# Keys, embedding and last norm turned by VectorE in 32x32 squares and moved between partitions by DMA through DRAM

## The chip, the cores and the metric

The kernel runs on one core of a Trainium2 chip. The metric is the device time of one execution in microseconds. All values are float32; matrix products are made of float32r pieces, each operand being split into a high part and a low part (the rest), with three products for one.

## What is computed

Eight samples of 512 tokens with 256 channels go through one gated block: an attention-free layer with a band of position biases, a two-layer network with 1024 hidden channels, and a gated token-shift network.

```python
def xattn(x, pos, wq, bq, wk, bk, wv, bv, wo, bo, pos_bias, gamma, beta, w1, b1, w2, b2):
    emb = x + pos
    q, k, v = emb @ wq + bq, emb @ wk + bk, emb @ wv + bv
    w = pos_bias * (abs(i - j) < 64)
    ek, ew = exp(k - max_over_tokens(k)), exp(w - max_of_row(w))
    y = sigmoid(q) * (ew @ (ek * v)) / (ew @ ek)
    a = layer_norm(y @ wo + bo + emb) * gamma + beta
    return layer_norm(relu(a @ w1 + b1) @ w2 + b2 + a) * gamma + beta
def ffn(x, W_r, W_k, W_v, mu_r, mu_k):          # x_prev is x moved by one token
    xr, xk = mu_r * x + (1 - mu_r) * x_prev, mu_k * x + (1 - mu_k) * x_prev
    return sigmoid(xr @ W_r.T) * (square(relu(xk @ W_k.T)) @ W_v.T)
x = x + tanh(g_xattn) * xattn(norm(x), ctx, ...)
x = x + tanh(g_ffn) * ffn(norm(x), ...)          # norm(x) here is "the last norm"
```

## The kernel before

Weights stay in SBUF. A sample is worked on in two layouts: rows (128 tokens on the partitions, four tiles of 256 channels) and channels (128 channels on the partitions, two chunks of 512 tokens). Three tensors per sample change layout on TensorE, with eight 128x128 transposes each, into PSUM:

- the embedding `emb`, rows to channels (`turn_emb`, L1444), for keys, queries and values. ScalarE takes the high part from PSUM (`emb_high`, L1097), VectorE the low part (`emb_low`, L588);
- the exponentials of the keys `ek_t` (the buffer of `y`), channels to rows (`turn_keys`, L1468), for the weighing by the band. ScalarE makes the high part (`ek_high`, L1114), VectorE the low part (`keys_low`, L634) and the product with the values (`weigh_values`, L639), both from PSUM;
- the last norm, rows to channels (`turn_fin`, L1599), which ScalarE copies to `xn_t` (`turned_copy`, L1131).

A fourth turn, of the middle norm, is not touched. The work is a software pipeline. `run_steps` (L303) writes out steps 1 to 7 for every engine. In step i four samples are in work: i in the attention and the first hidden chunks, b = i-1 in the last hidden chunks and the sum, a = i-2 in the token-shift network, d = i+1 in embedding, keys, queries and values; e = i+2 is being loaded and normed. Each engine has its own order written by hand in its `step` (SyncE L392, GpSimd L508, VectorE L879, ScalarE L1253, TensorE L1695), and an instruction waits for semaphores, with everything behind it on its engine. There is no planner.

In TensorE's step the order is: the weighing of the keys (`weigh`, part 0), the embedding's turn for d, the weighing of the values with a hidden chunk inside, `ffn_k` of a, keys of d, `ffn_r`, hidden chunks 2 and 3 of b with the output projection between, `ffn_v`, sums of the second layer, the middle norm's turn, queries of d, hidden chunks 0 and 1 of i, values of d, the keys' turn, a sum of the second layer, and the last norm's turn for b. VectorE begins with `sums_low`, the first reciprocal, `sums_low` again, the mix `xk` of a, `emb_low`, the second reciprocal and the mix `xr`. SyncE's queue holds in each step the second load of x, loads of x and the context for e, and the store of a. TensorE begins a step only with `ek_hi` and `val` of that sample.

GpSimd makes the low parts of `xr` and `y` and adds a row to `emb` in between (`xr_low`, `emb_plus_bo`, `y_low`). ScalarE's `exp_keys` of d writes the buffer of `y`, so it waits for `y_low`, and `hidden_high` of b's chunk 2 comes behind it.

Of the kernel before, what the change touches and what calls it, by code (L numbers as in the profile page):

```python
# [1 line left out]

# [24 lines left out]
FIN_DVE = 3  # L27
FIRST_DVE = 2
NU = 8

# [17 lines left out]
def flamingo_gated_block(nc, A_x, A_ctx, A_vec, A_rows, A_far, A_pos, A_wk, A_wq, A_wv, A_wo,  # L48
# [14 lines left out]
    with ctx:  # L63
# [82 lines left out]
        def pair(k):  # L146
# [52 lines left out]
                                                                   sem("sq_lo_done"), sem("tanh_r_done"))  # L199
        gated_done, out_done = sem("gated_done"), sem("out_done")  # L200
        last_norm_dve, last_sq_lo = sem("last_norm_dve"), sem("last_sq_lo")

# [38 lines left out]
        def sq_low(eng, n):  # L241
            low(eng, sq_lo, xk, sq_hi, sq_hi_done, n + 1, sq_lo_done)

        def make_emb(eng, n, p):
# [103 lines left out]
        def _(sp):  # L348
# [16 lines left out]
            def store(n):  # L365
                sp.wait_ge(out_done, n + 1)
                sp.dma_start(rows_of(out, n), out_sb.rearrange("p (b a d) -> p b a d", b=1, a=TT)).then_inc(out_stored, 16)

            load_x(0)
            load_ctx(0, 0)  # L370
# [41 lines left out]
        def _(pool):  # L412
# [43 lines left out]
            def emb_plus_bo(n, p):  # L456
                pool.wait_ge(emb_turned, n + 1)
                pool.wait_ge(rows_landed, 16 * 6)
                add_row(emb[p], bo_rows, emb_bo_done)
# [48 lines left out]
            def step(i, p):  # L508
# [19 lines left out]
                if has(e):  # L528
                    make_emb(pool, e, p)
                stats("ff", b)  # L530
                stats("fin", b)

            run_steps(pool, step)
# [33 lines left out]
        def _(dve):  # L567
# [71 lines left out]
            def weigh_values(n):  # L639

                dve.wait_ge(val_done, n + 1)
                dve.tensor_tensor(val, pair(0), val, ALU.mult).then_inc(ev_done, 1)

# [17 lines left out]
            def recip(n, c):  # L661

                dve.wait_ge(den_done, DC * n + c + 1)
                dve.wait_ge(exp_q_done, DC * n + c + 1)
                if c == 0:
                    dve.wait_ge(ek_turned, n + 1)
# [75 lines left out]
            def mix_k(n, chunks=range(DC)):  # L742

                mixed(n, xk, C_MUK, xk_done, chunks)

            def mix_r(n, chunks=range(DC)):

                mixed(n, xr, C_MUR, xr_done, chunks)

# [129 lines left out]
            def step(i, p):  # L879
# [25 lines left out]
                hidden_low(b, 3)  # L905
                if is_last(i):
                    normalise_mid(i)
                if has(a):
                    gate_ffn(a)
                if not is_last(i):  # L910
                    normalise_mid(i)
                if has(a):
                    make_out(a)
# [3 lines left out]
                ff_stats(b, None if is_last(i) else lambda: a_low(i))  # L917
                scale_ff(b)
                finish_x1(b)
                fin_stats(b)  # L920
# [3 lines left out]
                if has(d):  # L924
                    keep_values(d)
                    keys_low(d)
                    weigh_values(d)
# [139 lines left out]
        def _(act):  # L1067
# [29 lines left out]
            def emb_high(n):  # L1097
                act.wait_ge(emb_turned, n + 1)
                act.activation(emb_hi, pair(0), ACT.Copy).then_inc(emb_hi_done, 1)  # L1099

# [13 lines left out]
            def ek_high(n):  # L1114
                act.wait_ge(ek_turned, n + 1)
                after(act, wo_done, n)
                act.activation(ek_hi, pair(0), ACT.Copy).then_inc(ek_hi_done, 1)

# [12 lines left out]
            def turned_copy(n):  # L1131
                after(act, xr_done, DC * n)
                for c in range(DC):
                    o = c * (T + 1) + 1
                    act.wait_ge(fin_turned, DC * n + c + 1)
                    act.activation(xn_t[:, o:o + T], bank(2, c), ACT.Copy).then_inc(xn_t_done, 1)

# [115 lines left out]
            def step(i, p):  # L1253
                a, b, d, e = i - 2, i - 1, i + 1, i + 2
                if has(d):
                    after(act, v_done, d)
                    emb_high(d)
# [27 lines left out]
                if has(d):  # L1285
                    ek_high(d)
                if not is_last(i):
                    turned_copy(b)
                if has(d):
# [69 lines left out]
        def _(pe):  # L1359
# [122 lines left out]
            def weigh(n, part, dst, hi, lo, lo_ready, done, between=None, ahead=None):  # L1482

                near(dst, 0, hi, (ew_hi, ew_lo), True)
                if part == 0:
                    pe.wait_ge(lo_ready, n + 1)
                    near(dst, 0, lo, (ew_hi,))
                    after(pe, xn_t_done, DC * (n - 1))
                    relus_read(NQ * (n - 1) + 2)
# [205 lines left out]
            def step(i, p):  # L1695
# [3 lines left out]
                weigh(i, 0, 1, ek_hi, ek_lo, ek_lo_done, den_done)  # L1699
                if has(d):  # L1700
                    turn_emb(d, 1 - p)
# [42 lines left out]
                if has(d):  # L1744
                    values(d)
                    turn_keys(d)
                if not is_last(i):
                    add_hidden(i, 0)
                    turn_fin(b)

# [141 lines left out]
```

## Time and profile before

| | us |
|---|---|
| three runs | 475.52, 475.59 (median), 478.38 |
| profiled execution, whole | 477.9 |
| its span | 476.2 |
| TensorE matmuls busy | 453.5 |
| VectorE busy | 391.8 |
| ScalarE busy | 239.6 |
| GpSimd busy | 259.4 |
| granted TensorE clock, mean | 0.996 of full speed |

Busy time counts instructions of an engine while they run, by the profiler's records; the span is the time from the first to the last of them, and the profiled execution's own time has a little around it. In the rows PE is TensorE, DVE VectorE, ACT ScalarE, POOL GpSimd and SP SyncE; an L-number is a line of the kernel before. Matmuls overlap in the pipeline, so the time that a group of them takes is read from the starts of neighbours, not from their durations.

### The profile page before, as it was taken

The page shows a single profiled execution, that of the slowest core. Times are in us where ns is not written, and L with a number is a line of the kernel's source. Part 1 is how long each engine was busy: PE and PEld are TensorE (multiplying, and loading weights), DVE is VectorE, ACT ScalarE, POOL GpSimd, SP SyncE. Part 2 cuts the span into 40 slices and gives each one's busy share as a digit, 9 for nine tenths or more (in the row PEclk, how much of TensorE's full clock was granted, in tenths as well). Part 3 has the DMA queues.
Part 4 walks back from the last instruction along what each step waited for, and adds up shares of the span by engine and source line. Part 5 has one row for each costly group of instructions (what it writes and reads, how often), then busy time and mean ns, then how long its engine had stood idle before and what let it go on. Part 6 is the DMA issues. An engine that isn't in the chain of part 4 may idle for free.

```text
span 476.2 us, 8229 instructions
## 1 busy us (share of the span) xinstructions
PE 453.5 (95%) x3080; PEld 412.4 (87%) x3080; DVE 391.8 (82%) x733; ACT 239.6 (50%) x372; POOL 259.4 (54%) x239
## 2 busy tenths in 40 slices
PE   7889989899999999999999999999999999999975
PEld 7779788779989898999989898899989898897975
DVE  4898879986959989598968989599867979489987
ACT  3582562645265634736356643735345543538253
POOL 2574843661587535971577634973567335953621
PEclk9999999989999999999999999999999999999999
DMA  8740410102001300022001210021000110011002
GB/s 265 267 132 8 144 50 2 44 12 79 1 1 63 114 3 0 1 89 89 1 1 45 94 41 1 1 89 44 1 2 0 51 39 1 1 45 45 2 0 89
DMA packets 21895, 23.35 MB, mean 49 GB/s; under 512 B 992, under 2 KB 20960, under 8 KB 21856
## 3 DMA queue, kind: packets, MB, share of 16 engines
q1 hardware_dynamic: 20768, 21.26, 13.7%
q10 hardware_dynamic: 1088, 1.57, 1.0%
q8 instruction: 24, 0.39, 0.3%
q14 instruction: 15, 0.12, 0.1%
HBM read 18.64 MB, written 4.19 MB: 48 GB/s over the span
## 4 chain that ended last, share of the span: by engine, by line
PE 43%; issue 19%; POOL 16%; DVE 14%; ACT 4%; DMA 2%; ACTq 0%; POOLq 0%; DVEq 0%
PE ps L1361 40%; DVE y L670 4%; POOL xk_lo L225 3%; POOL hid_lo L225 3%; PE ps L1367 2%; POOL a_rows L434 2%; DMA hid<-in_wo 2%; DVE xk L738 1%; PE ps L1376 1%; POOL emb L434 1%; POOL ek_lo L225 1%; POOL ev_lo L225 1%; POOL x_beta L434 1%; DVE y L667 1%; DVE hid_lo L814 1%
## 5 line engine op out<-in xcount | busy, mean ns | idle before, releaser
L1361 PE MATMUL ps<-w_hi,hid_hi 128*128 128x256 f32 x288 | 72.2, 288 | 0.8 <-issue 0.5
L1361 PE MATMUL ps<-w_lo,hid_hi 128*128 128x256 f32 x288 | 70.6, 281 | 0.0
L814 DVE SCALAR_TENSOR_TENSOR hid_lo<-ps,neg_b,hid 128x512 fp32r<-128x512 f32 x60 | 41.3, 739 | 34.5 <-ACT hid L1190 34.5
L1361 PEld LDWEIGHTS ps<-w_hi,hid_hi 128*128 128x128 f32 x288 | 54.2, 188 | 3.5 <-DVE y L677 2.2
L1361 PEld LDWEIGHTS ps<-w_lo,hid_hi 128*128 128x128 f32 x288 | 54.3, 189 | 0.1
L670 DVE RECIPROCAL y<-y 128x512 f32<-128x512 f32 x16 | 53.7, 3353 | 0.6
L1361 PE MATMUL ps<-a_hi,w_hi 128*128 128x512 f32 x128 | 50.8, 397 | 1.1 <-DVE hid_lo L814 1.1
L1361 PE MATMUL ps<-a_hi,w_lo 128*128 128x512 f32 x128 | 50.7, 396 | 0.0
L1184 ACT ACTIVATE hid_hi<-ps,b 128x512 fp32r<-128x512 f32 x60 | 37.9, 686 | 24.8 <-PE ps L1361 24.8
L225 POOL TENSOR_TENSOR ev_lo<-res,ev_hi 128x1024 fp32r<-128x1024 f32 x8 | 19.1, 2383 | 51.7 <-ACT ev_hi L1129 51.7
L1361 PE MATMUL ps<-w_hi,hid_lo 128*128 128x256 f32 x288 | 41.6, 284 | 3.4 <-DVE hid_lo L814 2.2
L1361 PEld LDWEIGHTS ps<-w_hi,hid_lo 128*128 128x128 f32 x288 | 37.1, 188 | 4.8 <-DVE hid_lo L814 2.4
L1190 ACT ACTIVATE hid<-hid_hi,neg_b 128x512 f32<-128x512 f32 x60 | 40.1, 725 | 0.0
L1361 PE MATMUL ps<-a_lo,w_hi 128*128 128x512 f32 x128 | 35.1, 396 | 0.0
L434 POOL TENSOR_TENSOR a_rows<-norm,gamma_rows 128x1024 f32<-128x1024 f32 x8 | 20.1, 2509 | 19.7 <-issue 17.3
L1361 PEld LDWEIGHTS ps<-a_hi,w_hi 128*128 128x128 f32 x128 | 24.0, 188 | 6.7 <-DVE hid_lo L814 1.6
L225 POOL TENSOR_TENSOR xk_lo<-xk,xk_hi 128x1024 fp32r<-128x1024 f32 x7 | 17.2, 2460 | 22.6 <-ACT xk_hi L1141 22.6
L1361 PEld LDWEIGHTS ps<-a_lo,w_hi 128*128 128x128 f32 x128 | 24.1, 188 | 5.8
L1361 PEld LDWEIGHTS ps<-a_hi,w_lo 128*128 128x128 f32 x128 | 24.1, 189 | 5.2
L1361 PE MATMUL ps<-emb_hi,w_hi 128*128 128x512 f32 x64 | 26.9, 420 | 0.5 <-ACT emb_hi L1099 0.5
L1361 PE MATMUL ps<-emb_hi,w_lo 128*128 128x512 f32 x64 | 25.6, 399 | 0.0
L225 POOL TENSOR_TENSOR hid_lo<-xr,hid_hi 128x1024 fp32r<-128x1024 f32 x5 | 12.1, 2410 | 22.5 <-ACT hid_hi L1148 22.5
(251 smaller groups left out, 1327.5 us busy)
## 6 DMA issues: line engine op xcount, KB each, us to landing
x_in<-in_x SPq DMA_DIRECT2D x8, 512.0 KB, 4.4
emb<-in_ctx SPq DMA_DIRECT2D x8, 512.0 KB, 3.5
x_beta<-in_x SPq DMA_DIRECT2D x8, 512.0 KB, 3.6
out<-out_sb SPq DMA_DIRECT2D x7, 512.0 KB, 2.9
hid<-in_w SPq DMA_DIRECT2D x2, 512.0 KB, 6.8
x<-in_pos ACTq DMA_DIRECT2D x1, 512.0 KB, 6.2
out_sb<-in_pos ACTq DMA_DIRECT2D x1, 512.0 KB, 7.1
x<-in_w SPq DMA_DIRECT2D x1, 512.0 KB, 4.0
```

The costliest lines, as they stand in the source:

```text
L225: eng.tensor_tensor(dst, src, f32(hi), ALU.subtract).then_inc(done, 1)
L434: pool.tensor_tensor(dst.rearrange("p (a d) -> p a d", a=TT), src.rearrange("p (a d) -> p a d", a=TT), r, op).then_inc(done, 1)
L667: dve.scalar_tensor_tensor(out=tile(y, c, T), in0=tile(gate_q, c, T), scalar=1.0, in1=bank(1, c), op0=ALU.add, op1=ALU.mult).then_inc(den_ ...
L670: dve.reciprocal(tile(y, c, T), tile(y, c, T)).then_inc(recip_done, 1)
L738: dve.scalar_tensor_tensor(out=tile(dst, c, T), in0=tile(out_sb, c, T), scalar=vec[:, mu + c:mu + c + 1], in1=xn_t[:, c * (T + 1):c * (T + ...
L814: dve.scalar_tensor_tensor(out=tile(lo, b, T), in0=bank(relu_pair(n, q), b), scalar=neg_b1[:, m:m + 1], in1=tile(shifted, b, T), op0=ALU.m ...
L1184: act.activation(tile(hi, b, T), bank(relu_pair(n, q), b), ACT.Relu, bias=b1[:, m:m + 1]).then_inc(hid_hi_done, 1)
L1190: act.activation(tile(shifted, b, T), f32(tile(hi, b, T)), ACT.Identity, bias=neg_b1[:, m:m + 1]).then_inc(hid_shifted, 1)
L1361: return pe.matmul(o, s, m, start=start, stop=stop, skip_group_check=True)
L1367: last = pe.transpose(bank(dst, c)[:, a * P:(a + 1) * P], src[:, D * a + c * P:D * a + (c + 1) * P], ident)
L1376: last = pe.transpose(tile(pair(dst), a)[:, c * P:(c + 1) * P], src[:, T * c + a * P:T * c + (a + 1) * P], ident)
```

## The change

- For the keys of samples 2 to 7, the embedding of samples 3 to 7 and the last norm of samples 0 to 5, TensorE's turn is gone. VectorE transposes 32x32 squares in two instructions of 128x512 each, which leaves every square in its own group of 32 partitions (`turn_key_squares`, `turn_emb_squares`, `turn_fin_squares`). SyncE then stores the 512 KB to a room in DRAM, waits until they are there, and loads them back with the groups of partitions exchanged (`spread`). The first samples and the last ones keep TensorE's turns.
- The squares lie in borrowed buffers: `xk` to `y` for the keys, `xk` to `xr` for the embedding, `hid[0]` to `hid[1]` for the last norm.
- The low parts of keys and embedding move from VectorE to GpSimd (`ek_low` between the statistics "ff" and "fin", `emb_low_of` behind them). ScalarE, VectorE and GpSimd read the landed squares with a pattern in runs of 32 columns.
- Orders: on ScalarE `turned_copy` is the first thing of the next step, `ek_high` stands ahead of hidden chunks 0 and 1, and `emb_high` behind the last norm. On VectorE `turn_key_squares` follows `hidden_low` of chunk 3, `turn_emb_squares` follows `scale_ff`, `turn_fin_squares` stands between `keep_values` and `weigh_values`; `gate_ffn` comes behind `normalise_mid` in every step. On SyncE `spread_keys`, `store`, `spread_emb` and `spread_fin` are the end of a step.

```diff
+SQ = 32
+NB = P // SQ
+BLK_EMB = 3
+BLK_EK = 2
...
+        ek_blocks, ek_square = xk, y
+        emb_blocks, emb_square = xk, xr
+        fin_blocks, fin_square = hid[0], hid[1]
+        def by_squares(ap):
+            return ap.rearrange("p (a x j) -> p x a j", a=NB, j=SQ)
+        def by_columns(ap):
+            return ap.rearrange("p (x a j) -> p x a j", a=NB, j=SQ)
...
+        def moved(n, first, last=BATCH):
+            return 16 * max(min(n + 1, last) - first, 0)
...
+            def spread(square, blocks, room, landed, loads):
+                k = next(order)
+                after(sp, landed, 16 * loads)
+                sp.dma_start(room.rearrange("(i a n) -> a i n", a=NB, i=SQ), blocks).then_inc(room_filled, 16)
+                sp.wait_ge(room_filled, 16 * k)
+                sp.dma_start(square.rearrange("p (a n) -> p a n", a=NB),
+                             room.rearrange("(i a b n) -> b (i a) n", a=NB, i=SQ, b=NB)).then_inc(landed, 16)
+            def spread_keys(n):
+                sp.wait_ge(ek_turned, turns(n, BLK_EK))
+                sp.wait_ge(ek_summed, DC * (n + 1))
+                spread(ek_square, ek_blocks, rooms[0], ek_landed, n - BLK_EK)
+            def spread_emb(n):
+                sp.wait_ge(emb_turned, turns(n, BLK_EMB))
...
+                    sp.wait_ge(gated_done, n - BLK_EMB)
+                spread(emb_square, emb_blocks, rooms[1], emb_landed, n - BLK_EMB)
+            def spread_fin(n):
+                sp.wait_ge(fin_turned, DC * (n + 1))
+                sp.wait_ge(hid_lo_done, 2 * (NQ * (n + 1) + 2))
+                spread(fin_square, fin_blocks, rooms[2], fin_landed, n)
...
+                if has(i + 1):
+                    spread_keys(i + 1)
                 if has(i - 2):
                     store(i - 2)
+                if has(i + 2):
+                    spread_emb(i + 2)
+                if not is_last(i):
+                    spread_fin(i - 1)
...
+                    dve.wait_ge(ek_landed, moved(n, BLK_EK))
+                    dve.tensor_tensor(by_columns(val), by_squares(ek_square), by_columns(val), ALU.mult).then_inc(ev_done, 1)
+            def turn_key_squares(n):
+                after(dve, sq_lo_done, n - 2)
+                dve.wait_ge(ek_done, DC * (n + 1))
+                for c in range(DC):
+                    dve.transpose(ek_blocks.rearrange("p (b x c i) -> p c b x i", b=NB, x=TT, c=DC)[:, c],
+                                  tile(ek_t, c, T).rearrange("p (x b i) -> p b x i", x=TT, b=NB)).then_inc(ek_turned, 1)
+            def turn_squares(blocks, src, done):
+                for c in range(DC):
+                    dve.transpose(blocks.rearrange("p (b c x j) -> p c b x j", b=NB, x=TT, c=DC)[:, c],
+                                  src.rearrange("p (x c b i) -> p c b x i", c=DC, x=TT, b=NB)[:, c]).then_inc(done, 1)
+            def turn_emb_squares(n, p):
+                dve.wait_ge(emb_done, n + 1)
+                dve.wait_ge(ek_landed, moved(n - 1, BLK_EK))
+                turn_squares(emb_blocks, emb[p], emb_turned)
+            def turn_fin_squares(n):
+                dve.wait_ge(norm_done["fin"], TT * (n + 1))
+                turn_squares(fin_blocks, norm, fin_turned)
...
             def mix_k(n, chunks=range(DC)):
+                dve.wait_ge(ek_landed, moved(n + 2, BLK_EK))
+                dve.wait_ge(emb_landed, moved(n + 3, BLK_EMB))
...
             def step(i, p):
                 a, b, d, e = i - 2, i - 1, i + 1, i + 2
-                if has(d):
+                if has(a):
+                    turned_copy(a)
+                if d < BLK_EMB:
                     after(act, v_done, d)
                     emb_high(d)
                 sums_high(i, 1)
...
                     exp_q(d)
+                    ek_high(d)
                 hidden_high(i, 0)
                 hidden_high(i, 1)
                 normalise("fin", b, x1)
-                if has(d):
-                    ek_high(d)
-                if not is_last(i):
-                    turned_copy(b)
+                if has(e):
+                    act.wait_ge(v_done, e)
+                    emb_high(e)
```

## Rows read from the trace of the kernel before

**Rows 1.** The page: busy us (share of the span) and instructions of an engine.
```profile
PE 453.5 (95%) x3080; PEld 412.4 (87%) x3080; DVE 391.8 (82%) x733; ACT 239.6 (50%) x372; POOL 259.4 (54%) x239
```
**Rows 2.** Busy time by stretch: one middle step; PE, PEld, DVE, ACT, POOL, clock, DMA.
```profile
224.90:279.40 54.50, 54.28 (x373) 49.58 (x372) 45.55 (x87) 28.14 (x44) 32.47 (x28) 1.00 0.12 40
```
**Rows 3.** Timeline of TensorE: start us, us, instruction; two step starts, the keys' turn, its successor.
```profile
224.13 0.34 PE L1361 MATMUL ps<-ew_hi,ek_hi 128*128 128x192 f32 x1
...
274.05 1.04 PE L1376 MATMUL ps<-ident,y 128*128 128x128 f32 x8
274.84 0.37 PE L1361 MATMUL ps<-w_hi,hid_hi 128*128 128x256 f32 x1
...
278.60 0.34 PE L1361 MATMUL ps<-ew_hi,ek_hi 128*128 128x192 f32 x1
```
**Rows 4.** The chain that ended last, in order of time: part of one middle step.
```profile
228.33 3.35 DVE y L670
...
241.23 2.42 POOL hid_lo L225
```
**Rows 5.** Groups by line and shape: busy us, mean ns; idle before.
```profile
L626 DVE TENSOR_REDUCE ek_sums<-y 128x4 f32<-128x512 f32 x16 | 10.1, 674 | 0.0
L225 POOL TENSOR_TENSOR ek_lo<-y,ek_hi 128x1024 fp32r<-128x1024 f32 x7 | 16.8, 2400 | 7.5 <-ACT ek_hi L1166 7.5
```
**Rows 6.** Timeline of VectorE through one middle step.
```profile
233.62 1.22 DVE L590 TENSOR_TENSOR emb_lo<-ps,emb_hi 128x1024 fp32r<-128x1024 f32 x1
234.76 0.68 DVE L667 SCALAR_TENSOR_TENSOR y<-gate_q,ps 128x512 f32<-128x512 f32 x1
...
238.74 1.32 DVE L738 SCALAR_TENSOR_TENSOR xr<-out_sb,vec,xn_t 128x512 f32<-128x512 f32 x2
...
251.59 1.41 DVE L814 SCALAR_TENSOR_TENSOR hid_lo<-ps,neg_b,hid 128x512 fp32r<-128x512 f32 x2 [4.92 <-ACT hid L1190]
...
257.71 1.38 DVE L814 SCALAR_TENSOR_TENSOR hid_lo<-ps,neg_b,hid 128x512 fp32r<-128x512 f32 x2
...
266.15 2.27 DVE L687 SCALAR_TENSOR_TENSOR x<-res,mv_ff,gamma_t 128x256 f32<-128x256 f32 x4
268.94 1.71 DVE L696 SCALAR_TENSOR_TENSOR x<-x,rs_ff,x_beta 128x256 f32<-128x256 f32 x4 [0.52 <-POOL rs_ff L427]
...
276.00 1.21 DVE L618 TENSOR_TENSOR res<-ps,bv_rows 128x1024 f32<-128x1024 f32 x1
```
**Rows 7.** Timeline of ScalarE, the same step and its end.
```profile
240.09 1.06 ACT L1148 ACTIVATE hid_hi<-xr 128x1024 fp32r<-128x1024 f32 x1 [5.84 <-DVE xr L738]
...
278.51 1.09 ACT L1136 ACTIVATE xn_t<-ps 128x512 f32<-128x512 f32 x2 [2.36 <-PE ps L1367]
```
**Rows 8.** Timeline of GpSimd, the same step.
```profile
229.73 2.04 POOL L259 TENSOR_TENSOR out_sb<-xn_t 128x512 f32<-128x512 f32 x2
...
245.97 2.39 POOL L225 TENSOR_TENSOR ek_lo<-y,ek_hi 128x1024 fp32r<-128x1024 f32 x1
```
**Rows 9.** DMA issues (KB, us to landing); the queue in 255.90 to 260.00 (packets, MB, share).
```profile
emb<-in_ctx SPq DMA_DIRECT2D x8, 512.0 KB, 3.5
out<-out_sb SPq DMA_DIRECT2D x7, 512.0 KB, 2.9
out<-y SPq DMA_DIRECT2D x2, 256.0 KB, 2.1
...
q1 hardware_dynamic: 528, 0.52, 40.3%
```
**Rows 10.** Timeline of VectorE: the end of step 1, and step 7's beginning.
```profile
94.01 1.38 DVE L814 SCALAR_TENSOR_TENSOR hid_lo<-ps,neg_b,hid 128x512 fp32r<-128x512 f32 x2
...
101.83 1.70 DVE L687 SCALAR_TENSOR_TENSOR x<-res,mv_ff,gamma_t 128x256 f32<-128x256 f32 x4
...
386.90 1.22 DVE L642 TENSOR_TENSOR res<-ps,res 128x1024 f32<-128x1024 f32 x1
...
410.52 1.41 DVE L814 SCALAR_TENSOR_TENSOR hid_lo<-ps,neg_b,hid 128x512 fp32r<-128x512 f32 x2 [4.93 <-ACT hid L1190]
```

More of the change, by code:

```diff
@@ L1 @@
 from contextlib import ExitStack
+from itertools import count
 import concourse.bass as bass
@@ L200, in flamingo_gated_block @@
         gated_done, out_done = sem("gated_done"), sem("out_done")
+        ek_landed, emb_landed, fin_landed = sem("ek_landed"), sem("emb_landed"), sem("fin_landed")
+        room_filled = sem("room_filled")
+        rooms = [nc.dram_tensor(f"room{k}", [P * PAIR], F32, kind="Internal").ap() for k in range(3)]
         last_norm_dve, last_sq_lo = sem("last_norm_dve"), sem("last_sq_lo")
@@ L242, in sq_low, with turns, ek_low, emb_low_of @@
             low(eng, sq_lo, xk, sq_hi, sq_hi_done, n + 1, sq_lo_done)
+        ek_blocks, ek_square = xk, y
[5 more added lines that the diff above has]
+            return ap.rearrange("p (x a j) -> p x a j", a=NB, j=SQ)
+        def turns(n, first):
+            return n + 1 + max(n + 1 - first, 0)
+        def moved(n, first, last=BATCH):
+            return 16 * max(min(n + 1, last) - first, 0)
+        def ek_low(eng, n):
+            low(eng, by_columns(ek_lo), by_squares(ek_square), by_columns(ek_hi), ek_hi_done, n + 1, ek_lo_done)
+        def emb_low_of(eng, n):
+            low(eng, by_columns(emb_lo), by_squares(emb_square), by_columns(emb_hi), emb_hi_done, n + 1, emb_lo_done)
         def make_emb(eng, n, p):
@@ L530, in step @@
                 stats("ff", b)
+                if has(d):
+                    ek_low(pool, d)
                 stats("fin", b)
+                if has(e):
+                    emb_low_of(pool, e)
             run_steps(pool, step)
@@ L664, in recip @@
                 dve.wait_ge(exp_q_done, DC * n + c + 1)
-                if c == 0:
+                if c == 0 and n < BLK_EK:
                     dve.wait_ge(ek_turned, n + 1)
@@ L885, in step @@
                     mix_k(a)
-                if has(d):
+                if has(d) and d < BLK_EMB:
                     emb_low(d)
@@ L918, in step @@
                 scale_ff(b)
+                if has(e):
+                    turn_emb_squares(e, p)
                 finish_x1(b)
@@ L925, in step @@
                     keep_values(d)
-                    keys_low(d)
+                if not is_last(i):
+                    turn_fin_squares(b)
+                if has(d):
                     weigh_values(d)
@@ L1097, in emb_high @@
             def emb_high(n):
-                act.wait_ge(emb_turned, n + 1)
-                act.activation(emb_hi, pair(0), ACT.Copy).then_inc(emb_hi_done, 1)
+                if n < BLK_EMB:
+                    act.wait_ge(emb_turned, n + 1)
+                    act.activation(emb_hi, pair(0), ACT.Copy).then_inc(emb_hi_done, 1)
+                else:
+                    act.wait_ge(emb_landed, moved(n, BLK_EMB))
+                    act.activation(by_columns(emb_hi), by_squares(emb_square), ACT.Copy).then_inc(emb_hi_done, 1)
             def exp_keys(n, src=1):
@@ L1114, in ek_high @@
             def ek_high(n):
-                act.wait_ge(ek_turned, n + 1)
                 after(act, wo_done, n)
-                act.activation(ek_hi, pair(0), ACT.Copy).then_inc(ek_hi_done, 1)
+                if n < BLK_EK:
+                    act.wait_ge(ek_turned, n + 1)
+                    act.activation(ek_hi, pair(0), ACT.Copy).then_inc(ek_hi_done, 1)
+                else:
+                    act.wait_ge(ek_landed, moved(n, BLK_EK))
+                    act.activation(by_columns(ek_hi), by_squares(ek_square), ACT.Copy).then_inc(ek_hi_done, 1)
             def sums_high(n, part):
@@ L1284, in step @@
                 normalise("fin", b, x1)
-                if has(d):
-                    ek_high(d)
-                if not is_last(i):
-                    turned_copy(b)
+                if has(e):
+                    act.wait_ge(v_done, e)
+                    emb_high(e)
                 if has(d):
@@ L1699, in step @@
                 weigh(i, 0, 1, ek_hi, ek_lo, ek_lo_done, den_done)
-                if has(d):
+                if d < BLK_EMB:
                     turn_emb(d, 1 - p)
```

32 lines of the change are left out of this document (21 added, 11 removed).

## The prediction

> **What bounds the kernel now.** I read the page first. TensorE is busy 453.5 of 476.2 us and VectorE 391.8 [rows 1], so one asks whether TensorE is short of work anywhere, and how far VectorE is behind it. One middle step says it: of 54.50 us TensorE is busy 54.28, VectorE 45.55, GpSimd 32.47 [rows 2]. Steps start on TensorE at 224.13 and 278.60 [rows 3], 54.47 us apart, and I take this one for all five middle steps (2 to 6). So TensorE sets the pace. The chain of waits then shows that it does so narrowly: in each middle step it leaves TensorE for VectorE's first reciprocal and comes back from GpSimd's split of `xr`, 13 us later [rows 4]. There is a second loop beside TensorE's, nearly as long, and its length is what the change touches.
>
> **What leaves TensorE.** The eight transposes of the keys take 0.79 us of its time (274.05 to 274.84) [rows 3]; the other two turns have the same eight 128x128 transposes, three turns in a middle step, and I price them alike. The change removes the keys for samples 2 to 7 (6), the embedding for 3 to 7 (5), the last norm for 0 to 5 (6): 17 x 0.79 = 13.4 us. A middle step loses 2.4, so TensorE alone would take 52.1 us per step and the whole 462.8.
>
> **What VectorE gets.** Per middle step six square transposes of 128x512. No row has one. Nearest are one-source passes of VectorE over 512 columns, 674 ns [rows 5]; I take 0.70 each, 1.4 a pair, from nothing less than half that (0.7 a pair, if two columns passed at once) to double (2.8, if four-byte squares went at half pace). It loses `emb_lo` and `ek_lo`, 1.2 us each, spaced 1.14 apart [rows 6]; GpSimd takes both at 2.4 each [rows 5], and has 22 us free in the step [rows 2]. The square-wise reads and writes of ScalarE and GpSimd keep runs of 32 columns; I cost them nothing, as the sizes stay; ScalarE, busy 28.14 of 54.50 [rows 2], would hide a tenth more on each, some 0.5 us a step, except where it stands in the loops below.
>
> **The first loop, without any DMA.** It runs from the start of TensorE's step to `keep_values` of the next sample, for which TensorE's next step waits. Before: 224.13 to 277.21, against 278.60, a slack of 1.39 us [rows 3, 6]. VectorE's first part, up to 240.06, loses `emb_lo`, 1.14. That advances the `xr` mix, ScalarE's copy at 240.09, GpSimd's three passes without a gap (241.23 to 248.36), ScalarE's `exp_keys` that waits for them, and `hidden_low` at 251.59, which waits for ScalarE [rows 6 to 8]. From there to 277.21 VectorE has one gap, 0.52. Into this go the pairs of the keys and the embedding, 2.8. So 53.08 - 1.14 - 0.52 + 2.8 = 54.2 us, against 52.1 of TensorE. TensorE's saving is thus nearly gone before a transfer is counted: 0.3 us per step remain.
>
> **The round trips.** Each moved tensor is written to DRAM, SyncE waits for that, then it is read back; all in SyncE's order. Shown are one store of 512 KB in 2.9 us and a load in 3.5 [rows 9]: 6.5 us with the second issue. But in all of them both sides have 128 rows outermost. Here the DRAM side has four blocks outermost, both ways. If a transfer is dealt out by its outermost dimension, four of sixteen engines carry it. The load used 40.3% of 16 engines over 4.1 us, 26.4 engine-us, which is 1.65 us on 16 and 6.6 on four, beside a fixed 1.85: 8.5 us. Stores of 256 and 512 KB take 2.1 and 2.9 [rows 9], so 1.6 us of 512 KB scale and 1.3 don't: 7.7 on four. Together 16.2. The write has runs of 4 KB in place of 1 KB, and four engines don't press each other, so I take 15.3. The bounds are 6.5 (all engines) and 16.2; inside the four-engine case the low end is 12.8 (three quarters of the engine time).
> The Trainium skill, page "DMA: Bandwidth & Descriptors", section "Why a DMA increments its semaphore by 16 and not by 1", says that a DMA takes the largest number of engines up to 16 that divides the slowest dimension of both sides. By that it is four here, and the sum is the 595 us below in place of 486; no row of before shows a transfer with another number than 16.
>
> **The second loop, through the last norm.** Count from the end of VectorE's norm turn. At F its squares have landed. In the new order ScalarE copies them (1.1 [rows 7]) before the `sums_r` copy of the same step, and VectorE's `sums_low` waits for that copy between the two reciprocals: so all of VectorE stands behind the transfer. Copy, difference on GpSimd (two of 1.0 [rows 8]) and mix end at F+3.6; second reciprocal with its product (4.0, 234.76 to 238.74) F+7.6; `xr` mix (1.3) F+8.9; ScalarE (1.1) F+10.0; GpSimd's three passes (7.15) F+17.2; from the start of `exp_keys` to `hidden_low` 3.1: F+20.3 [rows 6 to 8]. Then 251.59 to 277.21 less 0.52 plus 2.8, 27.9: F+48.2; the norm turn 1.4: F+49.6.
> With F = 6.5 a step is 56.1, 1.6 longer than before. With four engines F is 15.3 and more: the embedding's turn ends only 9.8 us ahead of the norm's (`finish_x1` to the norm's turn: 268.94 to 277.21, and 1.4), its read back is then under way on the same four engines, and the norm's write waits some 3.3 us for it. F = 18.6.
>
> **The keys' wait.** Their turn ends 7.5 + 1.4 us after `hidden_low` at 251.59 (the hidden chunk at 257.71, 1.38 [rows 6]), F+29.2, and they land at F+44.5. VectorE comes to the embedding's turn, which waits for that landing, after `scale_ff` (268.42 in the old row, 16.8 after 251.59, and 1.4): F+38.5. With 15.3 it stands 6.0 us; with 6.5 not at all. Behind it on VectorE are `finish_x1`, the last norm and `hidden_low`, for which TensorE's second layer waits. ScalarE's `ek_high`, now ahead of both hidden chunks, waits for the same landing and adds nothing beyond it. GpSimd's `ek_low` stands ahead of the last norm's statistics, and is done by then. SyncE holds `store` behind the keys' write, which nobody needs before the next step.
> Step: F + 49.6 + 6.0 = 74.2 us, 19.7 more than 54.47.
>
> **The sum.** Five middle steps x 19.7 = 99. Step 1 has no norm to wait for, but the keys: `hidden_low` ends at 95.4, plus 1.4 and 15.3 is 112.1, against 103.5 + 1.4 for `scale_ff`, 7.2 us, and some 1 for the two turns net of idle time: 8 [rows 10]. Step 7 waits for the norm only: from its turn to `hidden_low` F + 17.9 (one pass of GpSimd less) = 36.5, against 23.6 before (386.90 to 410.52): 13 [rows 10]. The tail keeps its TensorE turn. 476.2 + 99 + 8 + 13 = 596 us of span. The profiled execution took 477.9, 1.7 more than its span, and the median of the runs is 475.59, 2.3 less than that: **595 us**. By 16.2 us (queueing 4.9, so F = 21.1 and a step of 77.6) it is 616; by 12.8 without queueing (a step of 65.9) 545.
>
> **Rivals.**
> (1) All 16 engines carry the squares: F = 6.5, no wait for keys. Five steps x 1.6, 1.5 in step 1 and 1 in step 7: 476.2 + 10.5, **487 us** on the median's scale 486. For it: every transfer shown runs so. Against it: the shape.
> (2) The norm's trip is hidden: if F is below 4.6, the first loop of 54.2 holds, and 5 x 0.3 is won: **474 us**, no change. For it: stores of 256 KB land in 2.1. Against it: two whole trips in series can't be shorter than 2.9 + 3.5 by these rows.
> (3) Faster, at **462 us**: TensorE's 13.4 us are all got back. The place is the run of VectorE from `hidden_low` to `keep_values`; the point is a pair of turns of 0.35 us or less (53.08 - 1.14 - 0.52 + 2 x 0.35 = 52.1), together with F below 2.5. For it: 17 sets of transposes do leave the engine that is 95% busy. Against it: no pass of VectorE over 512 columns is that short [rows 5].
> (4) Double-priced turns (2.8 a pair) with 16 engines: 4.2 more per step, 56.1 becomes 60.3, five steps 29, some 6 at the ends: about **511 us**. It fills the gap between (1) and the forecast.
>
> **Chances.** Four engines, 0.70, own range 545 to 620; (1) 0.13 and (4) 0.05; (2) 0.07; (3) 0.05. The range that holds the time 8 times in 10 must reach from the forecast down to (1): 484 to 620. A measurement of this kernel can tell 1% from no change. Faster 0.05, no change 0.07, slower 0.88.
>
> **What would show it.** In the changed kernel's DMA list the store to the room and the load from it: near 7 and 8 us each (four engines) or 3 and 3.5. On VectorE idle time ahead of `sums_low` of the second part, ended by ScalarE, some 12 us a step or 2, and ahead of the embedding's transposes, ended by a DMA, 6 or none. Steps of TensorE 74 us apart (or 56). The turns at 0.7 us. TensorE's busy time down by some 13 us. I am wrong if `xn_t` is written before TensorE's second weighing begins, or if the turns cost under 0.2 us.

## The result: 38% slower

The changed kernel takes 659.0 us (median of four runs, 657.66 to 660.98) beside 476.8 for the kernel before (475.52 to 478.38): a ratio of 1.382, 95% interval 1.375 to 1.389. The forecast was 595 us with a range of 484 to 620. The direction was right, and the time lies outside the range.

The page after, with the engines' busy time (answers [rows 1]), the granted clock in forty slices, and the chain that ended last by engine and by line:

```profile
PE 491.5 (75%) x2944; PEld 443.6 (67%) x2944; DVE 414.7 (63%) x756; ACT 238.2 (36%) x372; POOL 285.7 (43%) x250
...
PEclk9999999576995669976799767898677997789999
...
DMA 42%; DVE 21%; issue 13%; POOL 11%; PE 7%; ACT 6%; ACTq 0%; DVEq 0%; SPq 0%; POOLq 0%
DMA room<-hid 11%; DMA room<-xk 11%; DMA hid<-room 10%; DMA y<-room 9%; PE ps L1486 6%; DVE hid_lo L921 3%; DVE x L800 2%; POOL xk_lo L233 2%; POOL emb L506 2%; POOL ek_lo L233 2%; POOL hid_lo L233 1%; DVE xk L842 1%; DVE ek_sums L702 1%; DVE xk L729 1%; DVE res L881 1%
```

The kernel has changed its bound. Before, TensorE was busy 95% of the span. Now 42% of the chain is DMA, and nearly all of it (11, 11, 10 and 9%) is the way to `room` in DRAM and back. TensorE has 136 matmuls fewer, the 17 x 8 of the forecast, and is yet busy 38 us longer: it waits and then runs at a lower clock (mean 0.854 of full speed, 0.996 before).

One middle step, busy time by stretch (answers [rows 2]; columns as there):

```profile
300.00:386.00 86.00, 60.13 (x349) 54.41 (x349) 49.77 (x91) 27.80 (x43) 37.17 (x30) 0.82 0.23 62
```

SyncE's issues in this step (room is the tensor in DRAM; x1 is one transfer). Each load waits for the store ahead of it, so the difference of two starts is the time of a store (answers [rows 9]):

```profile
300.00 0.81 SPq L408 DMA_DIRECT2D room<-hid  x1
312.23 0.53 SPq L410 DMA_DIRECT2D hid<-room  x1
...
353.67 0.53 SPq L408 DMA_DIRECT2D room<-xk  x1
363.66 0.54 SPq L410 DMA_DIRECT2D y<-room  x1
...
374.42 0.54 SPq L408 DMA_DIRECT2D room<-xk  x1
384.44 0.52 SPq L410 DMA_DIRECT2D xr<-room  x1
```

The keys' store takes 10.0 us and the embedding's 10.0; the norm's, issued at 300.00 while the embedding's load is still under way, takes 12.2. In step 7 no embedding is moved, and the same store takes 9.99 (issued at 555.80, its load at 565.79). VectorE in the same step (answers [rows 6]):

```profile
325.51 0.42 DVE L763 TENSOR_TENSOR sums_r<-ps,sums_r 4x256 fp32r<-4x256 f32 x1 [11.06 <-ACT sums_r L1241]
...
352.35 1.29 DVE L729 STREAM_TRANSPOSE xk<-y 128x512 f32<-128x512 f32 x2
...
373.09 1.31 DVE L734 STREAM_TRANSPOSE xk<-emb 128x512 f32<-128x512 f32 x2 [10.00 <-DMA y<-room]
374.32 3.72 DVE L800 SCALAR_TENSOR_TENSOR x<-x,rs_ff,x_beta 128x256 f32<-128x256 f32 x4
...
384.52 1.29 DVE L734 STREAM_TRANSPOSE hid<-norm 128x512 f32<-128x512 f32 x2
385.74 1.18 DVE L722 TENSOR_TENSOR res<-y,res 128x1024 f32<-128x1024 f32 x1
```

Two waits stand where the forecast had put them: 11.06 us ahead of the second `sums_low` (behind the norm's trip) and 10.00 us ahead of the embedding's turn (for the keys' landing). And `finish_x1`, 1.71 us in [rows 6], now takes 3.72. ScalarE (answers [rows 7]) takes the norm's squares at 324.06 and the keys' at 373.08:

```profile
324.06 1.15 ACT L1257 ACTIVATE xn_t<-hid 128x512 f32<-128x512 f32 x2 [14.15 <-DMA hid<-room]
...
373.08 1.06 ACT L1234 ACTIVATE ek_hi<-y 128x1024 fp32r<-128x1024 f32 x1 [12.31 <-DMA y<-room]
```

The queue during one store of the keys (267.4 to 277.4; packets, MB, share of 16 engines), which answers the last row of [rows 9]:

```profile
DMA packets 132, 0.52 MB, mean 52 GB/s; under 512 B 4, under 2 KB 4, under 8 KB 132
...
q1 hardware_dynamic: 132, 0.52, 18.3%
```

128 packets of 4 KB carry the data, and four small ones signal the end. In the load of [rows 9] there were 512 of data and 16 small ones: one for each engine that took part. So this transfer ran on four engines of sixteen: a transfer whose outermost dimension is 8 or 2 leaves 8 or 2 small packets (experiment 1). The Trainium skill has this rule, as the forecast quoted it ("DMA: Bandwidth & Descriptors", section "Why a DMA increments its semaphore by 16 and not by 1"), and adds that each engine taking part writes the semaphore once; this trace agrees, with its 4 small packets.

### The profile page after: what moved, and what is told of

Read it like the earlier page. It is cut to its first block, busy times and chain, and to the rows that moved or that the text cites. A ratio compares the mean times of both kernels' runs of the same rounds, so it can differ in the third digit from the quotient of the medians.

```text
span 659.3 us, 8055 instructions
## 1 busy us (share of the span) xinstructions
PE 491.5 (75%) x2944; PEld 443.6 (67%) x2944; DVE 414.7 (63%) x756; ACT 238.2 (36%) x372; POOL 285.7 (43%) x250
## 4 chain that ended last, share of the span: by engine, by line
DMA 42%; DVE 21%; issue 13%; POOL 11%; PE 7%; ACT 6%; ACTq 0%; DVEq 0%; SPq 0%; POOLq 0%
DMA room<-hid 11%; DMA room<-xk 11%; DMA hid<-room 10%; DMA y<-room 9%; PE ps L1486 6%; DVE hid_lo L921 3%; DVE x L800 2%; POOL xk_lo L233 2%; POOL emb L506 2%; POOL ek_lo L233 2%; POOL hid_lo L233 1%; DVE xk L842 1%; DVE ek_sums L702 1%; DVE xk L729 1%; DVE res L881 1%
## 5 line engine op out<-in xcount | busy, mean ns | idle before, releaser
L1486 PE MATMUL ps<-w_hi,hid_hi 128*128 128x256 f32 x288 | 80.4, 310 | 46.7 <-ACT hid_hi L1307 45.9
L1486 PE MATMUL ps<-w_lo,hid_hi 128*128 128x256 f32 x288 | 78.7, 302 | 0.0
L233 POOL TENSOR_TENSOR ek_lo<-y,ek_hi 128x1024 fp32r<-128x1024 f32 x13 | 31.0, 2385 | 73.5 <-ACT ek_hi L1234 66.0
L1486 PE MATMUL ps<-ew_hi,ev_hi 128*128 128x192 f32 (+1 forms) x64 | 23.7, 382 | 50.9 <-DVE sums_r L763 50.7
L1486 PEld LDWEIGHTS ps<-w_lo,hid_hi 128*128 128x128 f32 x288 | 61.3, 213 | 0.3
L1486 PEld LDWEIGHTS ps<-ew_hi,ev_hi 128*128 128x128 f32 x64 | 18.1, 283 | 53.2 <-DVE sums_r L763 52.1
L1486 PEld LDWEIGHTS ps<-w_hi,hid_lo 128*128 128x128 f32 x288 | 40.2, 204 | 14.7 <-DVE hid_lo L921 14.3
L293 POOL TENSOR_TENSOR out_sb<-xn_t 128x512 f32<-128x512 f32 x12 | 12.2, 1039 | 70.6 <-ACT xn_t L1257 70.6
L233 POOL TENSOR_TENSOR emb_lo<-xr,emb_hi 128x1024 fp32r<-128x1024 f32 x5 | 11.8, 2360 | 66.1 <-ACT emb_hi L1212 66.1
L1257 ACT ACTIVATE xn_t<-hid 128x512 f32<-128x512 f32 x12 | 6.9, 623 | 86.2 <-DMA hid<-room 86.2
L1486 PE MATMUL ps<-far_c,sums_r 68*128 68x512 f32 x32 | 16.0, 591 | 28.5 <-DVE sums_r L763 28.5
```

What stands on the lines that cost most here:

```text
L233: eng.tensor_tensor(dst, src, f32(hi), ALU.subtract).then_inc(done, 1)
L293: eng.tensor_tensor(tile(out_sb, c, T), xn_t[:, o + 1:o + 1 + T], xn_t[:, o:o + T], ALU.subtract).then_inc(delta_done, 1)
L1257: act.activation(by_columns(xn_t[:, o:o + T]), fin_square.rearrange("p (a c x j) -> p c x a j", a=NB, c=DC, j=SQ)[:, c], ACT.Copy).then_in ...
L1486: return pe.matmul(o, s, m, start=start, stop=stop, skip_group_check=True)
```

## The experiments

**1. The transfers by themselves.** A kernel that only moves 512 KB, one transfer at a time, with 128, 16, 8, 4 and 2 blocks outermost; it computes nothing else.

```diff
+def store(outer):
+    go((room.rearrange("(i a n) -> a i n", a=outer, i=P // outer), src))
```

> No layer is computed, the output is a constant. SyncE issues stores and loads of 512 KB one after the other and waits for each: 8 stores of the output (128 rows outermost, runs of 1 KB), then twice a store to the room with 128, 16, 8, 4 and 2 blocks outermost in DRAM (runs of 4 KB), twice the same loads, twice the changed kernel's load (4 outermost, runs of 1 KB), twice the four loads of 32 partitions. Theory A: stores of 3 us for 128 and 16, some 5.5 for 8, 10 for 4, 18 for 2; loads 3.5, 3.5, 5.5, 9, 17. Rival B: the same time, 8 to 10 us, for every count, for stores to the room and loads from it.

SyncE's issues, each waiting for the one before; stores with 128, 16, 8, 4 and 2 blocks:

```profile
25.47 0.34 SPq L86 DMA_DIRECT2D room<-src  x1
28.11 0.64 SPq L86 DMA_DIRECT2D room<-src  x1
31.93 0.68 SPq L86 DMA_DIRECT2D room<-src  x1
37.86 0.54 SPq L86 DMA_DIRECT2D room<-src  x1
47.86 0.50 SPq L86 DMA_DIRECT2D room<-src  x1
60.61 0.33 SPq L86 DMA_DIRECT2D room<-src  x1
```

The stores take 2.64, 3.82, 5.93, 10.0 and 12.75 us. Loads of the same shapes took 3.15, 4.67, 6.80, 7.93 and 12.46; the second round of both agrees within 0.25 us. Theory A holds down to four blocks, give or take 1.3 us, and fails for two, where 18 and 17 us were expected. Rival B, one time for every count, is out. The change's own load (runs of 1 KB, four blocks outermost) took 10.27 and 9.14, and four loads of 32 partitions each, in its place, 4.26 together:

```profile
165.46 0.52 SPq L86 DMA_DIRECT2D dst<-room  x1
...
175.73 0.52 SPq L86 DMA_DIRECT2D dst<-room  x1
...
184.87 0.33 SPq L86 DMA_DIRECT2D dst<-room  x1
...
189.13 1.25 SPq L86 DMA_DIRECT2D dst<-room  x3
```

The shape alone makes the time; no other work is needed. This kernel ran once. A round trip on four engines is 10.0 + 9.1 to 10.3, so 19 to 20 us. The forecast had 15.3, with 16.2 as its upper bound.

**2. All sixteen engines.** The room is laid out row by row; the store has 128 rows outermost, and four loads of 32 partitions do the exchange. Everything else is as in the changed kernel.

```diff
-sp.dma_start(room.rearrange("(i a n) -> a i n", a=NB, i=SQ), blocks)
+sp.dma_start(room.rearrange("(p n) -> p n", p=P), blocks)
...
+for b in range(NB):
+    sp.dma_start(square[SQ * b:SQ * (b + 1)].rearrange("p (a n) -> p a n", a=NB),
+                 room.rearrange("(a i b n) -> b i a n", a=NB, i=SQ, b=NB)[b])
```

> The room in DRAM is laid out row by row, so the store has 128 rows outermost on both sides; the load is four loads, one for each group of 32 partitions, with 32 rows outermost on both sides. All else as in the changed kernel. Theory A (four engines carry each 512 KB, and three waits stand in line behind it): a store of 3 us and four loads of 5 together, F = 8, no wait for the keys, a middle step of 57 to 58 us in place of 86, in all about 495 us (485 to 510). Rival B (a trip through DRAM is slow by itself, however many engines carry it): each trip stays near 19 us and the time above 620. Rival C (TensorE's lower clock, 0.85 on average, is the cost, not the waits): above 560.

Measured: 503.4 us, a ratio of 1.055 (1.052 to 1.059), inside theory A's 485 to 510 and far below both rivals. I call this kernel version 2, and that of experiment 3 version 3. The store and the first of its loads, and what is left of the wait for the norm (in total, times, longest):

```profile
292.06 0.34 SPq L408 DMA_DIRECT2D room<-hid  x1
294.72 1.73 SPq L411 DMA_DIRECT2D hid<-room  x4
```
```profile
ACT xn_t L1258 <- DMA hid<-room: 25.8, 6, 5.3
```

The store takes 2.66 us in place of 12.2, and ScalarE waits 25.8 us for the norm over the whole kernel in place of 86.2. Of the 182 us that the change cost, 156 went with the shape of the transfers: four engines in place of sixteen, and blocks in place of rows. The remaining 27 us needed another cause.

**3. Hardly any data.** The changed kernel with one store and one load, 128 rows outermost, for each tensor. Only an eighth of it is moved, and the squares aren't exchanged, so the output isn't the reference's.

```diff
+sp.dma_start(room.rearrange("(p n) -> p n", p=P)[:, 0:P], blocks[:, 0:P])
...
+sp.dma_start(square[:, 0:P], room.rearrange("(p n) -> p n", p=P)[:, 0:P])
```

> Moves only the first 128 of 1024 columns of each tensor (64 KB, 128 rows outermost) and does not exchange the groups of partitions, so most of what the later layers read is stale; VectorE's turns, the moved low parts and all orders are the changed kernel's. It prices everything but the transfers. Theory A: two transfers of 2 us, F = 4.2, so the first loop of 54.2 us holds: 474 to 480 us. If instead the turns or the strided reads cost more than their rows, or the orders alone make a loop longer: 490 and more. If VectorE has room after all: 463.

Measured: 492.1 us (1.031; 1.027 to 1.035). Theory A failed, and the time is that of the alternative, 490 and more: even with almost nothing to move the kernel is 15.5 us slower. One middle step takes 58.35 us, against 54.2 by the forecast's first loop. Two things of this trace weren't in any sum, while the turns kept their price (1.30 us a pair, L733). `finish_x1` took 3.44 us here too. And TensorE, which waits at the end of a step for `keep_values`, starts the next step slowly. First its rows, then busy time and clock behind the wait:

```profile
283.36 1.21 PE L1486 MATMUL ps<-w_hi,hid_lo 128*128 128x256 f32 x8 [1.42 <-DVE hid_lo L920]
286.87 0.50 PE L1486 MATMUL ps<-ew_hi,ek_hi 128*128 128x192 f32 x1 [2.30 <-DVE res L693]
```
```profile
286.70:291.70 5.00, 4.83 (x23) 4.83 (x24) 2.76 (x5) 1.52 (x3) 1.33 (x2) 0.50 0.17 45
291.70:292.70 1.00, 1.00 (x7) 0.95 (x7) 0.00 (x0) 0.94 (x2) 1.00 (x1) 0.80 1.05 374
292.70:297.70 5.00, 5.00 (x44) 4.96 (x43) 4.84 (x4) 0.38 (x1) 3.27 (x3) 1.00 0.35 119
```

TensorE waits 1.42 us, works for 1.2 and waits 2.30. In the five microseconds behind that the granted clock is 0.50, the 1.2 GHz level, and then it is 1.00. The first matmul takes 0.50 us where [rows 3] have 0.34. VectorE's read of the first weighing (L770) begins 5.9 us after the step's start in place of 3.5.

**4. Filling TensorE's wait.** As 3, with matmuls of a constant, which nobody reads, ahead of the wait; first 24, then 10.

```diff
 add_hidden(i, 0)
+for _ in range(24):
+    mm(bank(0, 0)[:, 0:P], ident, ident, True, True)
```

> The version that moves an eighth of the data (its turned blocks are not exchanged, so the output isn't the reference's; 492 us), with 24 matmuls of a constant that nobody reads put before TensorE's wait for keep_values at the end of each step. Theory A (the wait drops the granted clock to the 1.2 GHz level for some 4.7 us, which costs 2.3 us a step): the clock stays at the 2.4 GHz level and the step loses 2.3 us: 478 us (474 to 483). Rival B (the slow start of the step has another cause): 492 us or more.

Measured: 500.6 us (1.050; 1.047 to 1.052). The 24 took 5.3 us, longer than the wait, and the step began that much later; but the clock was 1.00, and L770 came 3.5 us into the step. So the clock half of theory A held and its time of 478 us didn't: the filler was too long.

> As the version with 24 idle matmuls at the end of each step (500.6 us), but with 10: they took 5.3 us where the wait was some 2.3 us, so 10 should take 2.2 us and end before keep_values does. An eighth of the data is moved, not exchanged, and the output isn't the reference's. Theory A (the clock stays at the 2.4 GHz level through the wait; the reads that follow start 3.5 us into the step, as with 24, and not 5.9): the step is 2.3 us shorter than without idle matmuls, 478 us in all (475 to 482). Rival B (the clock falls all the same, or the step is set by VectorE): 489 to 493 us.

Measured: 483.9 us (1.015; 1.014 to 1.017), against 492.1 without filler and 478 (475 to 482) expected. The start of the same stretch of a step:

```profile
281.00:286.00 5.00, 4.93 (x42) 4.68 (x41) 4.12 (x6) 1.40 (x2) 2.72 (x2) 1.00 0.07 20
```

A middle step is 55.8 us (VectorE's L721 at 227.27 and 283.07) in place of 58.35. The clock's part of this step is therefore 2.5 us. Step by step (2 to 6) version 3 takes 55.79, 57.35, 58.35, 58.15 and 57.61 us at a mean granted clock of 1.00, 0.95, 0.94, 0.94 and 0.96; with ten matmuls it is 56.23, 55.78, 55.80, 55.80 and 55.24, all at 1.00. The first of them follows a wait of only 1.1 us and loses nothing. So four steps lose 1.6 to 2.6 us, the total fell by 8.2 us; the 14 expected is 2.3 us for six steps. What is left of a step over the 54.2 of the first loop is 1.6 us, and `finish_x1` is longer by 1.7 (3.43 us here, 1.71 in [rows 6]).

**5. GpSimd's pass beside VectorE's.** Version 2, with GpSimd's `ek_low` behind the last norm's statistics.

```diff
 stats("ff", b)
-if has(d):
-    ek_low(pool, d)
 stats("fin", b)
+if has(d):
+    ek_low(pool, d)
```

> The version with all three moved and every transfer on sixteen engines (503 us), with GpSimd's low part of the keys put behind the finish of the first state. Theory A (VectorE's finish took 3.4 us in place of 1.7 because GpSimd read memory beside it): it falls to 1.7 us again, and the step by 1.7: 492 us (488 to 497). Rival B (the finish is long because of the DMA traffic or its own operands): it stays at 3.4 us and the time at 503, or above it by what the later keys cost.

Measured: 499.0 us (1.047; 1.043 to 1.051), above theory A's 488 to 497 and below rival B's 503. `finish_x1` fell to 1.63 us (280.81), as theory A has it. The step went from 58.5 to 58.05 only. The durations of single instructions tell why (minimum, median, maximum in ns, then first and last start); `finish_x1` in version 2, then the last norm in this one:

```profile
L801 DVE SCALAR_TENSOR_TENSOR x<-x,rs_ff,x_beta x4: 474/477/2255, 280.8 to 283.8; 128x256 f32<-128x256 f32 x4
```
```profile
L824 DVE TENSOR_SCALAR norm<-x,rs_fin,nmr_fin x3: 402/402/1731, 286.8 to 288.8; 128x256 f32<-128x256 f32 x3
```

And GpSimd's `ek_low` in version 2, then in this one:

```profile
280.38 2.41 POOL L233 TENSOR_TENSOR ek_lo<-y,ek_hi 128x1024 fp32r<-128x1024 f32 x1
```
```profile
286.04 2.36 POOL L233 TENSOR_TENSOR ek_lo<-y,ek_hi 128x1024 fp32r<-128x1024 f32 x1
```

One instruction of each group is long, and it ends 0.1 to 0.3 us after GpSimd's: 280.81 + 2.25 = 283.06 beside 280.38 + 2.41 = 282.79, and 286.82 + 1.73 = 288.55 beside 288.40. The others have their ordinary time. So VectorE isn't slowed; it stands until GpSimd's instruction is over. Moving that instruction moved the stop to the norm, and won back 0.5 us of 1.8. The Trainium skill ("SBUF — State Buffer", section "SBUF: two separate sides") says that VectorE and GpSimd share a pair of ports that is locked for a whole instruction, where VectorE reads two SBUF operands or is in a two-port mode, and that the other then blocks fully. The trace agrees for two SBUF operands: 2255 ns in place of 477, to the end of GpSimd's instruction. The norm reads one and is stopped too, 1731 in place of 402; whether it runs in such a mode no row shows.

The kernel before had shown the stop already. The first half of the state's finish (L687) takes 2.27 us in [rows 6] and 1.70 in [rows 10]. In the first case the first of its four instructions, which starts at 266.15, takes 1080 ns and the others 471, and GpSimd is in this pass until 266.95; at 101.83 GpSimd's pass is just over.

```profile
264.54 2.41 POOL L248 TENSOR_TENSOR emb<-x_in,emb 128x1024 f32<-128x1024 f32 x1
```

**6. Only some of the three.** The norm back on TensorE, keys and embedding on four engines:

> The last norm is turned by TensorE again, with the copy where it was before; keys and embedding go through DRAM as in the changed kernel, with four blocks outermost. Theory A: the wait of VectorE for the keys (10 us) stays in six steps, and ScalarE's copy of the embedding, which lands some 20 us after its turn, now stands alone ahead of the first sums copy, 10 us in five steps: 575 to 600 us. Rival D (the norm's trip is the whole loss, the others lie beside other work): under 510 us. Rival E (all three add up singly, a third of 182 us each): about 598, which this run does not tell from A; the run with the norm alone does.

Measured: 600.9 us (1.259; 1.255 to 1.265), 0.9 above theory A's range and near rival E's 598; rival D is out. VectorE waits 9.58 us for the keys, and 12.17 behind the embedding's squares, where theory A has its two waits:

```profile
345.57 1.31 DVE L732 STREAM_TRANSPOSE xk<-emb 128x512 f32<-128x512 f32 x2 [9.58 <-DMA y<-room]
...
370.52 0.42 DVE L761 TENSOR_TENSOR sums_r<-ps,sums_r 4x256 fp32r<-4x256 f32 x1 [12.17 <-ACT sums_r L1237]
```

Then the norm alone on four engines:

> Keys and embedding stay on TensorE; only the last norm takes the change's way through DRAM on four engines. Theory A (a step is the norm's round trip plus the second loop, both as the changed kernel's rows price them, and the rest of a step is TensorE's own): store and load of the norm about 21.8 us (no embedding read queues before it), 47.9 us of work behind it, 0.65 us of longer mix: 70.4 us a step, 572 us in all (555 to 585). Theory B (each move adds what it adds alone to a kernel that TensorE bounds, so that the moves are a sum): the changed kernel is 183 us over the kernel before, the version with norm back on TensorE 124, so the norm alone is worth 59: 536 us (525 to 545).

Measured: 570.4 us (1.196; 1.192 to 1.199), theory A within 2 us; theory B's 536, and with it the plain sum of rival E, is out. Its middle steps take 70.4 us (L711 at 115.30 and 396.94, four steps). The parts don't add up: the norm alone costs 93 us and the other two 124, all three together 182. They stand in one loop, so part of the one wait can hide in the other; which part, these runs don't show.

**7. The embedding alone, on sixteen engines,** the one part with time enough for its trip.

> Only the embedding is turned by VectorE and moved, its store with 128 rows outermost and its loads 32 partitions each; keys and norm stay on TensorE. Theory A (the TensorE loop bounds the step and loses one group of turns of 0.79 us on five steps, the embedding's trip ends long before it is wanted): 472.5 us, 0.8% faster (470 to 475). Rival B (the two turns and the longer reads of VectorE, or a clock that pauses on TensorE where it waits for VectorE, take it back): 476 to 480 us.

Measured: 480.8 us (1.008; 1.006 to 1.010). Theory A is out; the time lies 0.8 above rival B's range. The new wait on TensorE, and GpSimd's two passes ahead of it:

```profile
233.22 0.69 PE L1482 MATMUL ps<-ev_lo,tile_rows 128*68 128x256 f32 x4 [1.73 <-POOL ev_lo L233]
```
```profile
228.45 2.40 POOL L233 TENSOR_TENSOR emb_lo<-xr,emb_hi 128x1024 fp32r<-128x1024 f32 x1 [6.40 <-ACT emb_hi L1207]
230.80 2.36 POOL L233 TENSOR_TENSOR ev_lo<-res,ev_hi 128x1024 fp32r<-128x1024 f32 x1
```

The embedding's low part stands ahead of that of the values, for which TensorE waits 1.73 us: more than the 0.79 of the turn that it lost. Yet this step is no longer than before, 54.44 us against 54.46, so the wait only eats the saving. The 3.6 us that steps 2 to 6 lose are mostly one step of 57.18 (169.01 to 226.19; 54.44 before). There the clock fell to 0.50 behind the same wait, as in experiment 3 and as rival B allows, and a matmul took 0.41 us in place of 0.28:

```profile
176.40 0.69 PE L1482 MATMUL ps<-ev_lo,tile_rows 128*68 128x256 f32 x4 [1.74 <-POOL ev_lo L233]
...
178.83 0.41 PE L1482 MATMUL ps<-w_hi,hid_hi 128*128 128x256 f32 x1
```

In the other four the wait is as long and the mean clock 1.00. The last version puts both new passes behind the values':

```diff
 ev_low(i)
 if has(a):
     delta_of(pool, a)
+if has(d) and d >= BLK_EMB:
+    emb_low_of(pool, d)
```

> The version that moves only the embedding (480.8 us), with ScalarE's high part of it put behind that of the values and GpSimd's low part behind delta_of, in the idle 2.6 us before xk_lo. Theory A (the low part of the embedding, 2.40 us, stood ahead of that of the values, ev_lo, for which TensorE waited 1.7 us a step): this wait goes, TensorE keeps its 0.79 us a step less of turning, and the time is 472.5 us, 0.9% under the kernel before (470 to 475). Rival B (the next thing is late instead: xk_lo on GpSimd, or VectorE's finish, with two turns more): 475 to 479 us.

Measured: 482.3 us (1.011; 1.010 to 1.013), outside both ranges (470 to 475, 475 to 479). TensorE's wait for `ev_lo` fell from 1.73 us to 0.7, as intended, but a new one of 0.9 us for `xk_lo` came in each step, as rival B names it, and the step is longer, 55.6 us (L715 at 225.41 and 281.00) against 54.4. GpSimd's pass in its new place, and the `xk` mix of VectorE beside it:

```profile
233.28 2.40 POOL L233 TENSOR_TENSOR emb_lo<-xr,emb_hi 128x1024 fp32r<-128x1024 f32 x1
```
```profile
L838 DVE SCALAR_TENSOR_TENSOR xk<-out_sb,vec,xn_t x2: 742/1628/2515, 233.7 to 236.1; 128x512 f32<-128x512 f32 x2
```

The first mix takes 2515 ns and the second 742: the stop again, 1.8 us, at another place. ScalarE's copy of the mix and `xk_lo` come behind it, and TensorE's new wait behind them. That all of the step's 1.1 us come from it wasn't tested. No version tried is faster than the kernel before.

## Why the forecast had the direction and missed the size

- **TensorE saves 13.4 us:** the 136 matmuls are gone. None of it was kept: no version was faster than the kernel before, and each one showed a wait for VectorE, GpSimd or a transfer.
- **A turn costs 0.70 us:** right. The three groups of the changed kernel (answers [rows 5]):

```profile
L729 DVE STREAM_TRANSPOSE xk<-y 128x512 f32<-128x512 f32 x12 | 7.8, 685 | 0.0
L734 DVE STREAM_TRANSPOSE hid<-norm 128x512 f32<-128x512 f32 x12 | 7.8, 686 | 0.0
...
L734 DVE STREAM_TRANSPOSE xk<-emb 128x512 f32<-128x512 f32 x10 | 6.5, 692 | 51.9 <-DMA y<-room 51.9
```

- **The first loop is 54.2 us:** with the transfers nearly gone and the clock kept up it is 55.8, and the stop beside GpSimd is as long as the 1.6 between them. The working held but for that; it took each engine's passes as if the other's didn't matter.
- **Four engines carry a transfer:** right, by 4 small packets and by experiment 1.
- **The round trip is 15.3 us, at most 16.2:** this term failed. It took 10.0 for the store (7.7 forecast) and 9.4 for the load (353.67 to 363.66 to 373.08; 8.5 forecast), 19.4 in all. I had split a transfer into a fixed part and a part that goes with the inverse of the number of engines. The rows behind it had 128 rows outermost, and experiment 1 shows that blocks cost more than rows on the same sixteen engines, 3.82 us and 2.64. The stores of 16, 8 and 4 blocks do lie near such a line (drawn through 3.82 and 10.0 it gives 5.9 for eight, measured 5.93), but not that of rows, nor that of two blocks (18.2, measured 12.75). I had also taken a discount for engines that don't press each other, for which no row spoke: the packets of the store on four engines took 29.3 engine-us (18.3% of 16 engines over 10.0 us), more than the 25.6 of the forecast (1.6 us on 16). That is 7.3 of the 10.0 us on each of four, and the 2.7 left are twice the fixed 1.3. And I had used the model's own spread as the bound. An upper bound should have come from a reason, not from the same model.
- **F = 18.6 us:** it was 24.1 (299.97, the end of the norm's turn, to 324.06), the same slower trip with 4.7 of queueing, against 3.3 forecast. The forecast's 3.3 had no working. Of the 4.7, 2.2 are in the store, beside the embedding's load; 2.4 are in the load, with two loads of x issued behind it, and their cause wasn't tested.
- **The keys' wait is 6.0 us:** measured 10.0. It is the trip of 19.4 less the work beside it, 9.4, which the forecast had as 9.3.
- **A step is F + 49.6 + keys' wait:** the form was right. With the measured terms and two that I had left out, `finish_x1` longer by 2.0 and the two `xk` mixes by 0.6 (2.08 us at 326.00), it gives 24.1 + 49.6 + 10.0 + 2.0 + 0.6 = 86.3; the step is 85.8 (L722 at 299.90 and 385.74). It is 11.6 us over the forecast's 74.2: 5.5 are F, 4.0 the keys' wait and 2.0 the stop beside GpSimd; 0.1 is left. Steps 2 to 6 together took 427.8 us, 57 more than five times 74.2. Step 1 adds 5 (13.3 us over the kernel before, 8 forecast) and the rest of the kernel 1 (14.3, 13 forecast). That makes 63 of the 64 us between 595 and 659.
- **Low parts on GpSimd are free:** the second step that failed, a cost put at nothing. GpSimd had 22 us free in the step, but a free engine isn't a free place. Its pass holds up VectorE's finish, norm or `xk` mix beside it by 1.3 to 2.1 us, and ahead of `ev_lo` it holds TensorE. The stop stood at L687 in [rows 6], and the forecast used both of its times (2.27 and 1.70) without asking why they differ.
- **Rival 1 (sixteen engines, 486 us):** when made so, it took 503. It lacked the two things that experiments 3 to 5 show, the stop, and TensorE's clock behind a wait of 2.3 us, and the 11 us between versions 2 and 3. Rivals 2 and 3 rested on hidden trips, and even an eighth of the data with sixteen engines wasn't enough.

The direction was no luck: the four engines, the two waits and the form of the step are as the traces show them. What failed is the price of a round trip and, less, that of GpSimd's passes.

Not settled: why a packet of 4 KB takes 0.23 us with four engines and 0.18 with two (29.3 and 23.1 engine-us for 128 packets), which is part of why four engines store in 10.0 us while two take only 12.75; and what makes up the 11 us between versions 2 and 3, of which steps 2 to 6 have 7.4.

## What to carry to other kernels

Look at the outermost dimension of a DMA on both sides before costing it; 128 rows outermost made the same 512 KB store in 2.6 us in place of 10. A wait in TensorE can cost more than itself, because its clock falls: 2.3 us did so in four steps here, 1.7 us in one of five. And before work is moved to an engine with idle time, find out what reads memory beside it: one GpSimd pass of 2.4 us cost VectorE or TensorE 1.3 to 2.1 us in four places, and nothing that shows in a fifth.

## What was not expected of the hardware

- A store of 512 KB took 2.64, 3.82, 5.93, 10.0 and 12.75 us with 128, 16, 8, 4 and 2 blocks outermost. Sixteen blocks of 32 KB are slower than 128 rows, by 1.2 us.
- A wait of 2.30 us in TensorE, 1.2 us of work after one of 1.42, was followed by 5 us at granted clock 0.50 (1.2 GHz). Ten idle matmuls in the wait kept it at 1.00. Behind a wait of 1.7 us the clock fell in one step and stayed at 1.00 in four.
- A VectorE instruction of 0.47 us took 2.25 when it began 0.4 us after a GpSimd pass of 2.41, and the three behind it took 0.47 again. GpSimd's pass kept its 2.4 us. Beside the pass of 289.66 to 292.02 in version 2 VectorE did an addition from PSUM (L695, 1.22 us) and the norm's turn (L735, 1.30), and neither was held up.
